# Earlier forget/input-gate rows for the first batches of a fused attention and spiking-MLP block, with new engine orders

## Time and profile before

| | us |
|---|---|
| median of three runs | 615.04 |
| lowest, highest | 613.74, 615.58 |
| the profiled execution | 614.5 |
| its span on the core | 612.7 |
| PE, DVE, POOL, ACT busy in the span | 569.9, 526.0, 494.1, 483.4 |

### The profile page before, as it was taken

The page is one execution under the profiler, slowest core; times in us unless marked ns, Lnnn a source line. Parts: engine busy times, 40 slices in busy tenths (PEclk is TensorE's granted clock), DMA queues, the critical chain, the costliest instruction groups (busy, mean ns, idle before and its releaser), DMA issues. The chain is left out here.

```text
span 612.7 us, 17703 instructions
## 1 busy us (share of the span) xinstructions
PE 569.9 (93%) x6032; PEld 477.4 (78%) x6032; DVE 526.0 (86%) x1291; ACT 483.4 (79%) x1009; POOL 494.1 (81%) x541
## 2 busy tenths in 40 slices
PE   1378989999999999999999999999999999999995
PEld 1267878788888888887888888888788888887894
DVE  7699899889999998989999898989999888867446
ACT  3667888888888788788888789788889777786673
POOL 6879889987997799987997889987997897955542
PEclk9985999999999999999999999999999999999998
DMA  8784727862574647651683736662685537601002
GB/s 276 194 145 119 149 77 129 186 126 83 108 189 87 160 77 127 168 157 55 106 183 91 161 72 125 175 151 61 106 176 124 85 55 143 120 3 36 0 1 70
DMA packets 72552, 71.33 MB, mean 116 GB/s; under 512 B 8080, under 2 KB 68112, under 8 KB 72464
## 3 DMA queue, kind: packets, MB, share of 16 engines
q1 hardware_dynamic: 71888, 70.00, 51.4%
q10 hardware_dynamic: 576, 0.21, 0.1%
HBM read 27.44 MB, written 8.39 MB: 58 GB/s over the span
## 5 line engine op out<-in xcount | busy, mean ns | idle before, releaser
L838 POOL TENSOR_TENSOR c_lo<-decay 128x512 bf16<-128x512 f32 x128 | 132.8, 1044 | 30.9 <-DVE decay L828 30.7
L1148 POOL TENSOR_TENSOR sq_lo<-w_raw,sq_hi 128x512 fp32r<-128x512 f32 (+1 forms) x96 | 111.9, 1167 | 39.1 <-ACT w_raw L1128 38.9
L1105 PE MATMUL z_ps<-x_hi,wfc_hi 128*128 128x512 f32 (+1 forms) x288 | 113.9, 395 | 1.5 <-ACT w_raw L1115 1.5
L1105 PE MATMUL z_ps<-x_hi,wfc_lo 128*128 128x512 f32 (+1 forms) x288 | 105.9, 368 | 0.0
L1105 PE MATMUL z_ps<-x_lo,wfc_hi 128*128 128x512 f32 (+1 forms) x288 | 105.6, 367 | 0.0
L1171 PE MATMUL y_ps<-sq_hi,wpr_hi 128*128 128x512 f32 (+1 forms) x256 | 103.2, 403 | 0.0
L1171 PE MATMUL y_ps<-sq_hi,wpr_lo 128*128 128x512 f32 (+1 forms) x256 | 96.8, 378 | 0.0
L1171 PE MATMUL y_ps<-sq_lo,wpr_hi 128*128 128x512 f32 (+1 forms) x256 | 96.6, 377 | 0.0
L828 DVE TENSOR_TENSOR decay<-qk_ps,decay 128x512 f32<-128x512 f32 x128 | 87.1, 680 | 9.0 <-ACT decay L820 6.0
L820 ACT ACTIVATE decay<-arg_ps,lqk_col 128x512 f32<-128x512 f32 x128 | 86.7, 677 | 9.8 <-PE arg_ps L797 8.6
L1189 DVE SCALAR_TENSOR_TENSOR spikes<-y_ps,spikes 128x1024 bf16<-128x1024 f32 (+1 forms) x64 | 73.8, 1153 | 1.2
(11 more groups left out here) (194 smaller groups left out, 1726.2 us busy)
## 6 DMA issues: line engine op xcount, KB each, us to landing
x_in<-x SPq DMA_DIRECT2D x32, 256.0 KB, 3.7
kT_in<-ctx_cols SPq DMA_DIRECT2D x32, 256.0 KB, 3.2
v_in<-ctx_rows SPq DMA_DIRECT2D x32, 256.0 KB, 4.4
k_stack<-kT_hi SPq DMA_DIRECT2D x64, 128.0 KB, 3.2
k_stack<-kT_lo SPq DMA_DIRECT2D x64, 128.0 KB, 3.7
q_stack<-qT_hi SPq DMA_DIRECT2D x64, 128.0 KB, 3.9
q_stack<-qT_lo SPq DMA_DIRECT2D x64, 128.0 KB, 4.2
out<-w_raw SPq DMA_DIRECT2D x32, 256.0 KB, 3.3
```

The costliest lines, as they stand in the source:

```text
L838: e.tensor_tensor(c_lo[i % NCH][:, :], c, top(c), ALU.subtract).then_inc(sem("c_lo"), 1)
L1105: ins = e.matmul(z_ps[:, tokens(q)], lhsT, rhs, start=(n == 0), stop=(n == len(terms) - 1))
L1148: e.tensor_tensor(sq_lo[n % NSQ][:, tokens(q)], relu[n % NRE][:, tokens(q)], sq_hi[n % NSQ][:, tokens(q)].bitcast(fp32), ALU.subtract).the ...
```

## The change

In `gate_cummax` the scan now signals by itself (`gate_max`), and `am_split` step 0 waits for that. The three bounds operations become `gate_bounds`, placed freely on DVE; for groups 0 and 1 they wait for split step 1 and read `m` from PSUM after it. The remainder of steps 1 to 3 of these two groups lies in `am_rest` (SBUF) as it does for the later groups, so the bank of `a` and `m` is not overwritten and is free for its next user when the bounds are done.

```
-            link(e, "vector", e.tensor_tensor_scan(m, a, b, LOWEST, ALU.max, ALU.max))
+            e.tensor_tensor_scan(m, a, b, LOWEST, ALU.max, ALU.max).then_inc(sem("gate_max"), 1)
+        def gate_bounds(e, g):
+            e.wait_ge(sem("gate_max"), g + 1)
+            if g < IN_PSUM:
+                e.wait_ge(sem("am_split"), 4 * g + 2)
             ... (row_max and the two halves of cs, as before; then_inc gate_cummax)
 am_split:
-                e.wait_ge(sem("gate_cummax"), g + 1)
+                e.wait_ge(sem("gate_max"), g + 1)
-            rest = am_of(g) if g < IN_PSUM else am_rest
+            src = (am_of(g) if n < 2 else am_rest)[0:r, :, :]
+        def load_rows(e, b):
+            for j, split in enumerate((1, 3, 4)):
+                e.wait_ge(sem("am_split"), 4 * g + split)
+                for rows, k, first in ((a_rows, 0, 0), (m_rows, 1, 3)):
+                    e.dma_start(rows[...first + j...], am_part[g % 2][row:row + NH, j, k, :])
```

More of the change, by code:

```diff
@@ L210, in misc_order @@
         def misc_order():
[L212 to L222, removed]
+            return [("q", 0), ("g", 0), ("gT", 0), ("q", 1), ("g", 1), ("q", 2), ("gT", 1), ("fT", 0), ("q", 3),
[13 rows of a table added]
         MISC_ORDER = misc_order()
@@ L1282, in sync_program @@
[L1282 to L1312, removed]
@@ new lines, in vector_program @@
+            ln3_stats(e, 7)
+            cmul(e, 9, 0)
+            ln3_offset(e, 7)
+            h_norm(e, 8)
+            ln2_stats(e, 8)
+            cmul(e, 9, 1)
+            q_lo(e, 13)
+            x1_step(e, 8)
+            cmul(e, 9, 2)
+            ln1_stats(e, 14)
+            ln3_stats(e, 8)
+            cmul(e, 9, 3)
+            x2_lo_step(e, 7)
+            ln3_offset(e, 8)
+            ln1_stats(e, 15)
+            state_own(e, 9)
+            spikes_step(e, 3, 0)
+            cmul(e, 10, 0)
@@ new lines, in vector_program @@
+            q_lo(e, 20)
+            state_own(e, 16)
+            ln3_stats(e, 15)
+            cmul(e, 17, 0)
+            ln3_offset(e, 15)
+            h_norm(e, 16)
+            ln2_stats(e, 16)
+            cmul(e, 17, 1)
+            q_lo(e, 21)
+            x1_step(e, 16)
+            cmul(e, 17, 2)
+            ln1_stats(e, 22)
+            ln3_stats(e, 16)
+            cmul(e, 17, 3)
+            x2_lo_step(e, 15)
+            ln3_offset(e, 16)
+            ln1_stats(e, 23)
+            state_own(e, 17)
@@ new lines, in vector_program @@
+            cmul(e, 20, 3)
+            q_lo(e, 24)
+            state_own(e, 20)
+            ln3_stats(e, 19)
+            cmul(e, 21, 0)
+            ln3_offset(e, 19)
+            h_norm(e, 20)
+            ln2_stats(e, 20)
+            cmul(e, 21, 1)
+            q_lo(e, 25)
+            x1_step(e, 20)
+            cmul(e, 21, 2)
+            ln1_stats(e, 26)
+            ln3_stats(e, 20)
+            cmul(e, 21, 3)
+            x2_lo_step(e, 19)
+            ln3_offset(e, 20)
+            ln1_stats(e, 27)
@@ new lines, in vector_program @@
+            x1_step(e, 23)
+            cmul(e, 24, 3)
+            q_lo(e, 28)
+            state_own(e, 24)
+            ln3_stats(e, 23)
+            cmul(e, 25, 0)
+            ln3_offset(e, 23)
+            h_norm(e, 24)
+            ln2_stats(e, 24)
+            cmul(e, 25, 1)
+            q_lo(e, 29)
+            x1_step(e, 24)
+            cmul(e, 25, 2)
+            ln1_stats(e, 30)
+            ln3_stats(e, 24)
+            cmul(e, 25, 3)
+            x2_lo_step(e, 23)
+            ln3_offset(e, 24)
```

1438 lines of the change are left out of this document (846 added, 592 removed), and 13 rows, old and new, of the table SLOTS.

## The result

The changed kernel takes 622.92 us (median of 4, 621.05 to 624.35) against 615.31 beside it: ratio 1.012, interval 1.0097 to 1.0143. Forecast were 610.3 us and a range up to 615.7. The profiled execution took 624.16 us, span 622.4.

What follows compares the result with a forecast made beforehand. PE bounds from 100 us on; before, a dependency chain to about 31 us, then DVE. DVE idle falling from 12.4 to 7.5, less 0.2, gains 4.7: 615.04 - 4.7 = 610.3 us, range 606.5 to 615.7.

Steps and rivals of the forecast that it cites:

- four signs of being wrong: `h_norm` of batch 1 after 56; clock below full after 60; PE idle over 2, 150-550; a later `arg` awaiting m-rows.
- Batch 0's chain: Start of the kernel: scan at 17.7, split step 0 at 18.5, first `arg` near 25.9, 4.9 us earlier.
- Behind `load_rows` now wait x of batches 4 and 5, k of 3 and 4: Transfers queued on SP in the start: DVE meets x of batch 4 as it lands, up to 0.5 us of wait.
- I count DVE's idle time and not the moved steps: DVE up to `h_norm` of batch 1: idle 7.5 us against 12.4, less 0.2 for waits, a gain of 4.7.
- The rearranged repeats: I price its new order at nothing, bounds -1 and +3 us over the span: POOL's new order in the repeated part: no cost, as POOL is busy 341.90 of 400 us.
- repeats lose: Rival: late rows of every fourth batch or POOL's order stall the dense PE, 5 us, about 615.5; chance 0.11.
- DVE swallows it: Rival: from 30 to 100 us, deferred statistics and bounds fill DVE; gain 0 to 1.8 us, about 614; chance 0.16.
- Low clock: Rival: a PE gap near 53 to 60 us brings full clock 15 us later; loss 1.9, 616.9 us; chance 0.11.
- upper bound: Largest gain worked out: batch 1's 6.4 us and 1.5 of the later idle, 7.9 us.

Runs made afterwards that it cites:

- new_start: The changed kernel's new orders up to about batch 7 on every engine, the old orders from there: 615.50 us, ratio to before 0.9999.
- early_k: The changed kernel with the k transfers of batches 3 and 4 issued ahead of the rows of batch 0: 620.49 us.
- psum_rest: New start with k of batches 3 and 4 early, old rest, and the old split of groups 0 and 1 (remainder in PSUM): 613.75 us.
- new_rest: The old orders up to about batch 7, the changed kernel's new orders from there: 623.70 us, ratio to before 1.0134.
- before_bounds: The orders of before with only the bounds of groups 5, 6, 7 and 9 moved back by three to five DVE calls: 620.05 us.
- bounds_back: The changed kernel with the bounds of groups 3 to 9 right behind the max scan on DVE: 622.62 us.
- clo_first: As psum_rest, with POOL's `split_wpr_lo(e, 0)` behind `c_lo_step(e, 0, 3)` in place of `c_lo_step(e, 0, 1)`: 615.47 us.
- hole: The changed kernel with POOL's high half of v behind the gate's split for batches 8 to 28: 623.69 us.

## Why the prediction was wrong

The forecast was off by 12.3 us of difference (-4.7 against +7.6). new_start splits that: the new start gave 0 where 4.7 us were forecast, and the rest cost 7.4 us more (622.92 - 615.50) where nothing was. Of the four signs of being wrong, three came: `h_norm` of batch 1 at 60.77, PE idle 5.9 us between 150 and 550, and a clock below full behind 85 us. No `arg` waited for late rows.

- *Batch 0's chain*: right to 0.2 us up to split step 0 (softplus 14.07, scan 17.66, step 0 18.42). Step 3, priced as its PSUM form with at most +0.4 us, took +1.5: the casts in the earlier trace rows that gave the bound are ACT's or read PSUM, none is an operation of DVE from SBUF to SBUF. First `arg` 26.73, not 25.9.
- *"Behind `load_rows` now wait x of batches 4 and 5, k of 3 and 4"*: the step looked at x alone and gave 0.5 us. For x it was right (landed 27.25 and 27.95). It was k that came late: issued at 25.4, usable at 32 to 34 us, and early_k takes the 3 us of idle away. This is the first failed step: 2.4 us of median (1.7 with the old rest).
- *"I count DVE's idle time and not the moved steps"*: the sum held DVE's busy time fixed at 45.28 us. It was 50.08. This is the second failed step: +4.8 us in the start, which with the 3.0 of idle makes the whole error of `h_norm` of batch 1 (60.77 - 53.0 = 7.8). The two terms are not independent, though. That the idle term fits with k early (7.8 against 7.7) is in part luck: with 2.7 us less DVE work psum_rest has 9.3 us of it, and no less time in all. What else keeps the start from the forecast is open.
- *"The rearranged repeats: I price its new order at nothing, bounds -1 and +3 us over the span"*: new_rest costs 8.1 us, up to 3.4 of them by the clock. The rival "repeats lose" named the late rows or POOL stalling PE, and had 5 us; PE's waits after 150 us name no transfer of rows; what it waits for are `spikes`, `decay` and `w_raw`. The step priced POOL by its load, and DVE's moved bounds not at all; it did not ask what stands beside DVE's scans and bounds, nor what is late behind them, when two to four calls slip in between. Four moved bounds alone cost 4 us (before_bounds). That is the largest term, and its other part stays open.
- *DVE swallows it* came nearest for the start by its number (about 614; new_start 615.5), not by its cause: DVE was stretched by 4.8 us, and stood idle 3.0 us more than forecast. *Low clock* did not come as described: the full rate returned about 3 us sooner, not later. But the clock fell at other places, behind waits of PE: at 85.3 in the changed kernel (at most 1.7 us), twice in new_rest (3.4 us).
- The stated range reaches down to 606.5, a gain of 8.5 us, while the upper bound worked out was 7.9 (607.1). It changes nothing here.

## What to carry to other kernels

An order is more than each engine's load and its waits: for each SBUF-to-SBUF operation of VectorE, look at which GpSimd instruction runs beside it before and after the change, and let it end up to 0.6 us after that one in the estimate. Where VectorE is what is full, sum its busy time anew and do not carry it over. Then follow what stands behind the stretched operation: bounds_back shows that shorter operations alone need not give time. Of a queue behind a new wait, ask for every item who is the first to need it, and take its time from loads that also had stack transfers around them (6.5 us and more here), not from the median of all.

## What was not expected of the hardware

- The scan of 256 columns takes 0.68 us free. In clo_first it takes 2.39 beside one GpSimd instruction of 2.36 that began 0.52 us sooner, and 3.28 (76.79 to 80.07) beside four GpSimd instructions that follow each other without a gap up to 79.53. Both times it ends about 0.55 us after GpSimd has stopped.
- The same scan takes 3.29 us in the changed kernel and 0.89 in hole, whose orders are the same up to there, although it begins 0.7 us after the same `c_lo` in both. In hole GpSimd pays instead: its next instruction takes 1.42 us in place of 1.06, and the two after that 0.92 and 1.10 in place of 0.76. Which of the two engines waits is not told by anything that these rows show.
- The Trainium skill ("SBUF — State Buffer", section "SBUF: two separate sides") describes a port pair of VectorE and GpSimd as an exclusive lock: an operation of VectorE with two SBUF inputs and one of GpSimd that reads SBUF do not run together, the later one waits until the other is through. The rows agree in the main (2.39 beside 2.36; forms with a PSUM operand kept their 473 and 677 ns in the changed kernel); four instructions waited out in one scan are more than that sentence says.
- Two k transfers of 0.25 MB each, issued from 25.4 us on, let POOL start on the second only 6.6 to 8.6 us later; the median for such a load on the page is 3.2. In the changed kernel that of batch 3 landed at 32.72, after three of the stack transfers of 0.13 MB issued behind it (30.89 to 32.55). In early_k the same two took 6.5 us with the eight stack transfers of batch 0 ahead of them and none right behind. So it is not shown that those behind make them slow; both times many transfers were under way.
